# Layer 0's attention in four 32-row quarters, search pairs beside the scores, expert stages by chunks

## The reference, cut to what matters

```
x = x + tanh(g_xattn[0]) * L0_xattn(layernorm(x), ctx, ctx)    # 32 heads of 4: softmax(q1 k1) v - lam * softmax(q2 k2) v,
                                                               # then rms-normalised per head, projected
x = x + tanh(g_ffn[0])   * L0_ffn(layernorm(x))                # top 2 of 8 experts, one shared expert, silu
x = x + tanh(g_xattn[1]) * L1_xattn(layernorm(x), ctx, ctx, mask)   # 16 heads of 8, masked softmax
x = x + tanh(g_ffn[1])   * L1_ffn(layernorm(x))                # top 2 of 8 experts, silu(h1) * h2
# attention: scores = q @ k.T * scale; attn = softmax(scores) @ v
# experts:   every expert for every token, then a sum weighted with the router's choice
```

## Time and profile before

| | us |
|---|---|
| median of 3 runs (2277.94 to 2285.57) | 2283.0 |
| the profiled execution | 2273.94 |
| its span, first to last instruction | 2272.1 |
| PE busy in the span | 2036.9 (90%) |
| DVE busy | 1702.4 (75%) |
| ACT busy | 1497.4 (66%) |
| POOL busy | 1273.1 (56%) |
| mean granted PE clock | 0.949 |

### The profile page before, as it was taken

How to read it: one execution, slowest core, us unless ns; L and a number is a source line. 1 busy time by engine, 2 the same in 40 slices (tenths; PEclk the granted TensorE clock), 3 DMA queues, 4 the chain that set the end, 5 groups by cost and what they waited for, 6 DMA issues and landing times. The chain is left out here.

```text
span 2272.1 us, 67374 instructions
## 1 busy us (share of the span) xinstructions
PE 2036.9 (90%) x27256; PEld 1260.1 (55%) x27256; DVE 1702.4 (75%) x3701; ACT 1497.4 (66%) x2101; POOL 1273.1 (56%) x1418
## 2 busy tenths in 40 slices
PE   3799999999999999999985985999999999998798
PEld 2344444444444444444443863567766776676576
DVE  3688888888888888888943554777777777774644
ACT  2168888888888888888773432577777777776322
POOL 5326556556556556556423444687777778771332
PEclk9589999999999999999997996799999999999799
DMA  3544453453443443444301015677767777761000
GB/s 101 129 84 109 93 112 108 95 112 107 95 112 107 95 112 107 95 112 108 67 2 54 25 31 120 141 157 146 155 140 147 154 153 152 144 141 37 33 1 16
DMA packets 95244, 227.82 MB, mean 100 GB/s; under 512 B 46308, under 2 KB 58852, under 8 KB 88292
## 3 DMA queue, kind: packets, MB, share of 16 engines
q1 hardware_dynamic: 94692, 223.67, 44.2%
q10 hardware_dynamic: 256, 0.00, 0.0%
HBM read 146.77 MB, written 76.48 MB: 98 GB/s over the span
## 5 line engine op out<-in xcount | busy, mean ns | idle before, releaser
L1081 ACT ACTIVATE probs<-score_ps 125x896 f32<-125x896 f32 x1152 | 1039.0, 915 | 309.4 <-PE score_ps L978 304.7
L1139 DVE TENSOR_REDUCE max_part<-max_ps 112x1 f32<-112x500 f32 x1024 | 663.6, 672 | 81.8 <-PE max_ps L949 43.0
L995 PE MATMUL acc_ps<-probs,vext 125*32 125x224 f32 (+1 forms) x12288 | 563.4, 312 | 4.5 <-issue 3.7
L978 PE MATMUL score_ps<-qstack,kstack 50*125 50x224 f16 (+1 forms) x6144 | 456.2, 249 | 72.4 <-ACT probs L1081 67.1
L978 PEld LDWEIGHTS score_ps<-qstack,kstack 50*125 50x125 f16 x6144 | 305.5, 134 | 310.5 <-ACT probs L1081 246.5
L949 PE MATMUL max_ps<-kstack,qstack 48*112 48x500 f16 x1536 | 460.5, 394 | 17.8 <-DMA kstack<-k_parts 12.9
L995 PEld LDWEIGHTS acc_ps<-probs,vext 125*32 125x32 f32 x12288 | 303.4, 110 | 188.8 <-issue 136.3
L1136 DVE CUSTOM_DVE_ANT_0 kstack<-max_ps,kstack 112x500 f32<-112x500 f32 x512 | 333.4, 675 | 84.1 <-PE max_ps L949 56.0
L1139 DVE TENSOR_REDUCE max_part<-spare_ps 112x1 f32<-112x500 f32 x512 | 344.5, 673 | 44.6 <-PE max_ps L949 42.9
L949 PE MATMUL spare_ps<-kstack,qstack 48*112 48x500 f16 x768 | 304.4, 396 | 18.7 <-issue 16.8
L1136 DVE CUSTOM_DVE_ANT_0 kstack<-spare_ps,kstack 112x500 f32<-112x500 f32 x256 | 172.8, 675 | 83.9 <-PE max_ps L949 80.9
(11 more groups left out here) (187 smaller groups left out, 2617.5 us busy)
## 6 DMA issues: line engine op xcount, KB each, us to landing
kstack<-k_parts SPq DMA_DIRECT2D x384, 187.5 KB, 6.4
k_parts<-khl SPq DMA_DIRECT2D x128, 375.0 KB, 2.9
ctx_f<-in_ctx SPq DMA_DIRECT2D x32, 750.0 KB
ctx_f<-context_parts SPq DMA_DIRECT2D x22, 750.0 KB, 8.0
context_parts<-ctx_f SPq DMA_DIRECT2D x16, 750.0 KB, 3.3
context_parts<-kstack SPq DMA_DIRECT2D x16, 750.0 KB, 3.3
mask_in<-in_mask SPq DMA_DIRECT2D x128, 82.0 KB
XnT<-context_parts SPq DMA_DIRECT2D x10, 750.0 KB, 8.2
```

The costliest lines, as they stand in the source:

```text
L978: last = nc.tensor.matmul(buf[0:KT, r, GC * k:GC * (k + 1)], kstack[n % SLOTS][rows, c, keys], qstack[n % SLOTS][rows, c, :], start=not L. ...
L995: last = nc.tensor.matmul(acc_ps[32 * j:32 * j + 32, TT * S * i:TT * S * (i + 1)].rearrange("p (s c) -> p s c", s=S), vext[n % SLOTS][:, c ...
L1081: nc.scalar.activation(probs[t % 2][:, 896 * h:896 * h + 896].rearrange("k (b c) -> k b c", b=2), score_ps[h][0:KT, :, 0:448], ACT.Exp, sc ...
L1139: nc.vector.reduce_max(best, scores, AX.X).then_inc(s_red, 1)
```

## The change

1. Layer 0's `kstack` and `qstack` are cut into four quarters of 32 rows: blocks of 8 rows, 24 (`krows`) and the two more rows, 112 columns a group. Half h of the scores takes quarters 2h and 2h+1 with all four column groups: 8 matmuls of 112 columns over 26 rows. Search matmuls have 24 rows; the numbers of pieces and their widths stay. `piece` is ordered so that a pair lies on the two quarters that the scores beside it don't use.
2. The order of a step in layer 0 is now: scores 0 with pair 0 issued ahead of their first matmul, the first half of `weigh`, scores 1 with pair 1, the second half of `weigh`, prepare.
3. DMAs for layer 0: constant rows 12 for 6, `load_q` 12 for 6, `fill_k` 12 for 6, `fill_m` 8 for 4, of half the rows each.
4. The weights' order in the projections is plain; two splits of 64 columns become one of 128.
5. Expert stages: chunks 1 to 3 are straight code; 6 router matmuls go ahead of the first expert and 10 behind its projection; the choice of experts is made in chunk 0 after expert 0, its exponential ahead of expert 2; X of a chunk is completed in the next chunk, at expert 2; in layer 1 each chunk is stored when it is complete.

```diff
-        self.group_dims = D // (2 * PAIRS)
+        self.tile = rows_per_tile
+        self.row_tiles = 128 // rows_per_tile
+        self.group_dims = D // (self.row_tiles * PAIRS)
+        self.krows = 3 * self.group_dims
...
-L0 = Layer("L0", 32, 4, False)
-L1 = Layer("L1", 16, 8, True)
+L0 = Layer("L0", 32, 4, False, HALF // 2)
+L1 = Layer("L1", 16, 8, True, HALF)
...
+              "each search pair inside the scores": ("scores and pair 0", "weigh 0", "scores and pair 1", "weigh 1", "prepare")}
 
     def order_of(n, t):
 
+        if not L.masked:
+            return ORDERS["each search pair inside the scores"]
...
-        r, third, c, i = p % 2, p // 2 % NTHIRD, p // (2 * NTHIRD) % PAIRS, p // (2 * NTHIRD * PAIRS)
-        return r, third, c, i, (r * PAIRS + c) * L.parts + i
+        if L.masked:
+            r, third, c = p % 2, p // 2 % NTHIRD, p // (2 * NTHIRD)
+        else:
+            turn = p // 4
+            r, third, c = 2 * (p // 2 % 2 ^ turn % 2) + p % 2, turn % NTHIRD, turn // NTHIRD
+        return r, third, c, r * PAIRS + c
...
-                half = L.tiles // 2
+                groups = L.tiles // ROW_TILES
                 for part in range(2):
-                    for r in range(2):
-                        row = HALF * r + KROWS + part
+                    for r in range(ROW_TILES):
+                        row = TILE * r + KROWS + part
                         sp.dma_start(qstack[n % SLOTS][row:row + 1, :, :].rearrange("a c q -> a (c q)"),
-                                     max_rows[half * r:half * (r + 1), part, 0:PIECE]).then_inc(s_mrow[n % SLOTS], 16)
+                                     max_rows[groups * r:groups * (r + 1), part, 0:PIECE]).then_inc(s_mrow[n % SLOTS], 16)
...
-                for k, c in enumerate(columns):
-                    for r in range(2):
-                        rows = slice(HALF * r, HALF * r + KROWS + 2)
-                        last = nc.tensor.matmul(buf[0:KT, r, GC * k:GC * (k + 1)], kstack[n % SLOTS][rows, c, keys],
+                for c in range(PAIRS):
+                    if c == SEARCH_AT and pair:
+                        search(pair)
+                    for b in range(2):
+                        r = 2 * h + b if H == 2 else b
+                        rows = slice(TILE * r, TILE * r + KROWS + 2)
+                        last = nc.tensor.matmul(buf[0:KT, b, GC * c:GC * (c + 1)], kstack[n % SLOTS][rows, c, keys],
...
             def chunk(c):
                 for e in range(NX):
                     up(c, e)
+                    if c == 0 and e == 0:
+                        route(range(FIRST_ROUTED, NTT))
                     if e:
                         down(c, e - 1)
                 down(c, NX - 1)
+            route(range(FIRST_ROUTED))
+            pe.wait_ge(s_w, 32)
             steps(pe, chunk)
...
+            def add_total(c):
+                dve.wait_ge(s_acc, (c + 1) * NX + 1)
+                k = slice(CH * c, CH * c + CH)
+                nc.vector.scalar_tensor_tensor(X[:, k, :], total[:, k, :], T["tg"][0:TT, 2 + layer:3 + layer], X[:, k, :],
+                                               ALU.mult, ALU.add).then_inc(s_res, 1)
...
+                    if c == 0 and e == 0:
+                        choose_experts()
+                    if c == 0 and e == 1:
+                        weigh_experts()
                     if e:
                         take(c, e - 1)
+                    if c and e == 2:
+                        add_total(c - 1)
```

More of the change, by code:

```diff
@@ L60, in __init__ @@
         self.parts = self.group_cols // PIECE
-        self.tiles = 2 * PAIRS * self.parts
+        self.tiles = self.row_tiles * PAIRS * self.parts
         self.pieces = self.tiles * NTHIRD
@@ L84, in unpacked @@
     return parts
-def halves_first(ap):
-    return ap.rearrange("p (h r x) -> p r h x", h=2, r=2)
 def key_order(layer, weight, *parts):
[L94 to L101, removed]
+    r = (L0, L1)[layer].row_tiles
+    return (weight.rearrange("p (r c d) -> p r c d", r=r, c=PAIRS),
+            *(x.rearrange("p (r d c) -> p r c d", r=r, c=PAIRS) for x in parts))
 def by_chunk(ap):
@@ L594, in order_of @@
             return ORDERS["both scores first"]
-        if L.masked and not busy[0]:
-            return ORDERS["scores apart by a pair"]
-        return ORDERS["scores apart by the product" if L.masked and busy[0] else "scores apart by the product" if busy[0] else "scores apart by the product"]
+        return ORDERS["scores apart by the product" if busy[0] else "scores apart by a pair"]
     turnaround = [("F", i) for i in range(L.uses_f)] + [("A", 0)]
@@ L981, in scores, with weigh @@
                 last.then_inc(s_scores, 1)
-            def weigh(n, t):
-                pe.wait_ge(s_exp, (n * STEPS + t + 1) * 2)
-                if t == 0:
+            def weigh(n, t, parts=range(2)):
+                if 0 in parts:
+                    pe.wait_ge(s_exp, (n * STEPS + t + 1) * 2)
+                if t == 0 and 0 in parts:
                     at_least(pe, s_os, n)
@@ L990, in weigh @@
                 for chunk, column in chunks:
-                    for i in range(2):
+                    for i in parts:
                         for j in range(4):
@@ L998, in weigh @@
                                 skip_group_check=True)
-                last.then_inc(s_av, 1)
+                if 1 in parts:
+                    last.then_inc(s_av, 1)
             turns = len(first_banks)
@@ L1027, in _ @@
                             scores(n, t, int(work[-1]))
+                        elif work in ("scores and pair 0", "scores and pair 1"):
+                            scores(n, t, int(work[-1]), searched(n, t, int(work[-1])))
                         elif work in ("pair 0", "pair 1"):
@@ L1031, in _ @@
                             weigh(*weighed)
+                        elif work in ("weigh 0", "weigh 1") and weighed[0] >= 0:
+                            weigh(*weighed, [int(work[-1])])
                         elif work == "prepare":
@@ L1226, in feed_forward @@
     AHEAD = 2
+    FIRST_ROUTED = 6
     def makes_parts(c, e):
[L1230 removed]
+        if c:
             return [], []
@@ L1260, in _ @@
                         sp.dma_start(mask_row[t], src[:, CH * c + t, :]).then_inc(s_mask, 16)
+        if layer == 1:
+            s_out = sem("result_stored")
+            @block.sync
+            def _(sp):
+                for c in range(NCH):
+                    sp.wait_ge(s_res, c + 1)
+                    sp.dma_start(out[CW * c:CW * c + CW, :].rearrange("(t p) d -> p t d", p=TT),
+                                 X[:, CH * c:CH * c + CH, :]).then_inc(s_out, 16)
+                sp.wait_ge(s_out, 16 * NCH)
         def before_hidden(c, u):
@@ L1266, in steps @@
         def steps(eng, body):
-            body(0)
-            with eng.Fori(1, NCH) as c:
+            for c in range(NCH):
                 body(c)
@@ L1273, in _, with route @@
         def _(pe):
-            for t in range(NTT):
-                last = nc.tensor.matmul(bank[7][0:TT, NE * t:NE * t + NE], XnT[:, TT * t:TT * t + TT],
-                                        small[f"routerT{layer}"][:, :], start=True, stop=True)
-            last.then_inc(s_lg, 1)
-            pe.wait_ge(s_w, 32)
+            def route(tiles):
+                for t in tiles:
+                    last = nc.tensor.matmul(bank[7][0:TT, NE * t:NE * t + NE], XnT[:, TT * t:TT * t + TT],
+                                            small[f"routerT{layer}"][:, :], start=True, stop=True)
+                if t == NTT - 1:
+                    last.then_inc(s_lg, 1)
             def project(ps, c, e, row):
```

146 lines of the change are left out of this document (68 added, 78 removed).

## The result

The changed kernel takes 2433.7 us (median of 4 executions, 2411.4 to 2454.0), beside 2281.7 for the kernel before on the same chip. Two of the four were slow ones (over 1.5% above the kernel's fastest); the ratios here leave such executions out, the medians keep them, and no profiled execution is one. The ratio is 1.058, 95% interval 1.054 to 1.062. The forecast was 2270 with a range of 2238 to 2308: the time moved the other way and lies far outside. The profiled execution took 2416.6 (span 2414.8).

What follows compares the result with a forecast made beforehand. Layer 0's batches were taken as bound by PE's step cycle, then by the chain of maxima; batches -6, start +4, setup -1, expert stages -10 make -13 us, giving 2270 us, range 2238 to 2308.

Steps and rivals of the forecast that it cites:

- The step of PE: Layer 0's steps: pair and scores together in 0.36, turn steps 2.66 us, 33.0 a batch by steps.
- Rival 2: Layer 0 scores wait for the search pair's end: 0.49, +0.5 us a batch, 2291 us; chance 0.15.
- Rival 3: Layer 0 scores and pair don't overlap: 0.55, +1.2 us a batch, 2312 us; chance 0.13.
- Value steps: Layer 0's three steps a batch with a value projection: 2.78 us each after the change.
- The chain of maxima: Layer 0: maxima for the next batch's scores, with eight copies taking 4.9, set the batch at 33.9 us.
- the sentence on the fills: Layer 0: the twelve key fills, wanted at step 7 (18.9 us into a batch), are hidden, so cost nothing.
- The sign of being wrong: Layer 0's batch period under 33 us (copies or POOL not late) or over 34.5 (no quarter overlap, or clock falls).
- Rival 4: Layer 0: waits at batch starts and in steps lower PE's clock, +1 us a batch, 2300 us; chance 0.09.
- Rivals 1 and 2: Layer 0: the first, full overlap and quick copies, 2240 us, 0.18 with its neighbour; the second, scores waiting, 2291, 0.15.
- not bound by the chain: Layer 0: maxima copies' landing hidden, steps alone decide, -1.1 us a batch, 2243 us; shares the chance 0.18.
- Layer 0's start: Before layer 0's first search: more constant rows and query loads delay the first key store, +4 us.
- Expert stages: Both layers' expert stages: earlier routing -5 us, later additions and result store by chunk -5, in all -10.

Runs made afterwards that it cites:

- wide early: Changed kernel with key fills as four DMAs of 8 rows and four of 16, and the maxima split and copied earlier: 2300.5 us, 1.0062.
- wide fills: Changed kernel with layer 0's key fills as four DMAs of 8 rows and four of 16 instead of twelve of 8, all bytes moved: 2322.5 us.
- half fills: Changed kernel, but from layer 0's fourth batch each key fill moves only the first half of each key row: 2315.0 us.
- busy tail: As wide early, plus two unread search matmuls beside each group of scores in layer 0's last 16 steps without a search: 2267.3 us, 0.9968.

## Why the prediction was wrong

*The step of PE: right.* Forecast 2.66 for turn steps with pair and scores together in 0.36. PE and DVE in the changed kernel:

```profile
646.52 0.41 PE L938 MATMUL spare_ps<-kstack,qstack 24*112 24x500 f16 x1
646.53 0.41 PE L938 MATMUL max_ps<-kstack,qstack 24*112 24x500 f16 x1
646.53 0.43 PE L971 MATMUL score_ps<-qstack,kstack 26*125 26x112 f16 x8
646.89 0.58 PE L989 MATMUL acc_ps<-probs,vext 125*32 125x224 f32 x8
647.41 0.41 PE L938 MATMUL max_ps<-kstack,qstack 24*112 24x500 f16 x1
647.71 0.41 PE L938 MATMUL spare_ps<-kstack,qstack 24*112 24x500 f16 x1
...
649.22 0.42 PE L938 MATMUL max_ps<-kstack,qstack 24*112 24x500 f16 x2
```

```profile
646.97 0.68 DVE L1138 TENSOR_REDUCE max_part<-spare_ps 112x1 f32<-112x500 f32 x1 [0.26 <-PE max_ps L938]
```

Together at 646.53, the product 0.36 behind (the earlier trace rows for before), the second piece held 0.30 until the reduce ends at 647.65, the next turn step 2.70 after this one. Rival 2's 0.49 is not what the rows show. The rule of the Trainium skill that was set beside it ("TensorE: Matmul & The Clock Gate", part 3, matmuls end in program order) would, worked out as rival 2 does, have given the 0.49; the trace does not agree with that time. Whether the ends kept their order it can't say, since a profile's ends of matmuls are modelled. Rival 3 falls too. Value steps were forecast 2.78 and are 2.9 to 3.1 (in wide early): about 0.4 a batch.

*The chain of maxima: right.* Forecast: POOL starts the output at +15.3, split done at +27.9, copies 4.9, next batch at +33.9. Measured in the changed kernel +15.53, +28.13, 4.91 (the earlier trace rows for before), and where only this binds, 34.14 to 34.6.

*The failed step is the sentence on the fills*: they "are wanted at step 7, 18.9: hidden". I counted the issues on SP (4.04 measured) and gave the transfer itself no price, though the kernel before showed 187.5 KB a DMA and a DMA share of 0.88 in that stretch, with the last landing near +13 of a deadline near +20. With half the rows in a DMA the landing went from about 11 us behind the first issue to 18 to 21, and PE's search had 20 waits of 1.3 to 4.3 us, with half clock behind them. The rows had the price: 96 packets of 1.57 us, 16 at a time, are 9.4 us, and 8 at a time 18.8 (an estimate from the packets; for wide fills it gives 12.6, and all three landings lie within 2.4 us of it). Wide fills, with every byte moved, gave back 110 us of the 147 between the forecast and the profiled execution; half fills gave back 97.

The sign of being wrong did come, a period over 34.5, but neither of the two causes set beside it (quarters that don't overlap, a clock that falls at the borders of the batches) was the one.

*Rival 4 had the mechanism in the wrong place.* It put +1 a batch on idle time at the border of a batch. The clock did fall, behind a wait of 3.6 us at step 7. Rivals 1 and 2, and "not bound by the chain", never came into play.

*The tail of layer 0* was in no term: +15.2, most of it at half clock, where the steps have scores and products only:

```profile
1303.00:1350.00 47.00, 45.91 (x470) 21.25 (x474) 0.36 (x2) 27.84 (x33) 6.90 (x13) 0.51 0.01 1
```

*Layer 0's start*: forecast +4, measured +12.4 to the first scores. The 8-row fills are part of it: on the kernel before they alone moved the first search by 5.9, and with wide fills 5 of the first search's 11 went again.

*Expert stages*: forecast -10, measured -15.2 in the trace; by themselves -13.6 in the medians and -11.5 in the trace. So that they beat the forecast is in part luck: 2.7 us of it is the moment at which the clock came up. In layer 1's stage the second projection starts 8.06 behind the router's start instead of 13.70, 5.6 sooner instead of 3; the 20 late records of the router take 2.04 at the clock that they meet there, where the forecast took 3.8 from rows at the lower one.

```profile
2270.82 2.38 PE L1286 MATMUL spare_ps<-wide,XnT 128*112 128x8 f32 x12 [1.19 <-PEq L343]
...
2276.98 2.04 PE L1286 MATMUL spare_ps<-wide,XnT 128*112 128x8 f32 x20
2278.88 0.54 PE L1294 MATMUL score_ps<-qh,kstack 128*128 128x448 f16 x2
```

*Layer 1's attention* (+8.7) stays open. First to last output copy is 633 to 636 in before and its three variants, and 636 to 646 in kernels made from the changed one, with the same work.

## What to carry to other kernels

When a tile gets narrower, look at every DMA that fills it, not only at the matmuls: at the same bytes and the same packets, rows per DMA decide how many DMA engines work (here 8 rows, 8 engines; 16 rows, 16), and a transfer that lands well ahead today has a deadline that should be written beside its landing time. A wait of a few microseconds on PE can be paid twice, here once as 3.6 us idle and once as 3.4 at half clock behind it. In a loop tied to several chains, measure the slack of each: here 1.4 us on the maxima, some 7 us on the fills, and the change spent both.

## What the hardware showed that I had not expected

- Half clock can be a steady state of a PE that is hardly ever idle: busy 60.02 of 60.12 us at 0.50, for 1956 us, while the same matmuls with scores and pairs on different row quarters ran at 1.00 in 33.70 us, busy 33.09.
- Four 32-row tiles work at once: two searches of 500 columns and eight score matmuls of 112 take 0.36 together, where the kernel before needs 0.24 and 0.30 one after the other.
- Where the steps had only scores and products, the clock was 0.50 from 1177 to 1230 us of wide early, with PE busy 51.68 us of these 53; two unread searches beside the scores brought it to 0.87 over the last 58 us.
- PE can stop for 4 to 5 us in the middle of a group that waits for nothing, as at 226.7 in the changed kernel (two matmuls of eight left):

```profile
226.12 0.58 PE L989 MATMUL acc_ps<-probs,vext 125*32 125x224 f32 x6
231.23 0.95 PE L989 MATMUL acc_ps<-probs,vext 125*32 125x224 f32 x2 [4.54 <-issue]
```

The traces say more on this. One DMA queue is of kind "instruction" and moves packets of 16 KB, about one in 9 us of layer 0. In this stop it has one, from 227.91 to 229.66, and PE goes on 1.6 us behind its end:

```profile
q8 instruction: 1, 0.02, 2.4%
```

All fourteen stops over 2 us in front of scores, products or turns in layer 0's attention (four in the changed kernel, ten in five kernels made from it) end 1.4 to 2.2 us behind the end of such a packet. That PE's instructions arrived late fits every one of them, though no run was made to test it. Why they should come late there, and why busy tail has as many of these packets and no such stop, stays open.
